# DLRM tower on one core: the first layer's dense part reads its features from the samples' slots instead of a contiguous copy

## The chip, the cores and the metric

One core of a Trainium2 chip. The metric is the device time of one launch in microseconds. Five engines work at once and meet only through semaphores: TensorE (PE, its weight loads listed apart as PEld), VectorE (DVE), ScalarE (ACT), GpSimd (POOL) and SyncE (SP, here only an issuer of transfers). 'us' is microseconds.

## What is computed

For each of 512 samples, 26 embedding rows of 128 numbers are looked up and put beside the sample's 128 dense features: 27 vectors. All pairwise dot products (351) and the dense features again go through three layers.

```python
combined = concatenate([e, dense[:, None, :]], axis=1)        # (512, 27, 128)
z = einsum('bfd,bgd->bfg', combined, combined)[:, triu_i, triu_j]   # 351 pairs
h = concatenate([z, dense], axis=1)                           # 479 features
h = maximum(h @ W_top1 + b_top1, 0)                           # 479 -> 512
h = maximum(h @ W_top2 + b_top2, 0)                           # 512 -> 256
y = h @ W_top3                                                # 256 -> 1
```

Everything is fp32.

## The kernel before

**Layout.** The samples go in four tiles of 128. `xt[d, tile, sample, slot]` holds the transposed vectors: on each of the 128 partitions (one for each feature number d), for each sample 32 slots of 4 bytes, of which 27 are used. Slot 0 is the dense vector, slots 1 to 16 the embeddings that are gathered from memory row by row, slots 17 to 26 those of ten small tables that are looked up by a matmul with a one-hot matrix. So the same slot of two neighbouring samples is 128 bytes apart. Within a tile a sample's place in `xt` is 4g + q, group inside quarter turned round: everywhere else (the transposed rows, the layers) it is 32q + g, with q in 0..3 and g in 0..31.

**The first half** (to about 58 us) is a loop over the ten one-hot tables (`for o in range(NO)` on every engine). The table comes by a transfer of SP (L267) into one of two buffers; the issue waits until DVE has finished with the table that was there (`low_ready`). ACT and DVE build the one-hot matrix out of PSUM (L375, L381, L476, L484). ACT rounds the table to its high part (L379), DVE makes the rest (L490), PE multiplies both (L627, L635), and ACT writes the picked 128 x 512 block into its slot of `xt` (L311). Meanwhile POOL issues 64 indirect gathers (L297). Behind the fourth table SP also issues the layers' weights, 1.5 MB (L272 to L277).

**The dense features** are loaded once (L270). PE transposes the four tiles into a PSUM bank behind the second table (L787). ACT, behind its work for the third table, copies the bank twice: into slot 0 of `xt`, turned into the order 4g + q (L394), and as it is into `dense_t`, 128 x 4 x 128 contiguous (L396). The second copy raises `dense_out`. PE waits for that before it uses the bank again, for the first transposes of gathered rows (`transposes`, L648).

**The second half** goes tile by tile, in an order written out by hand in PE's block (L796 to L836), with the other engines' lists beside it. For each tile: `transposes` (L650) turns gathered rows, ACT and DVE put them into `xt`; `gram` (L670) multiplies each pair of samples' slots with themselves, in four sets of 64 records; ACT (L325) and DVE (L523) take the results out; DVE transposes them by 32 x 32 blocks (L533), both pack the triangle's columns densely (`pack`, L355, L358, L540), PE transposes back (`back`, L693; for the last tile `back_last`, L706), ACT and DVE copy (L330, L545). Then come the first layer's 384 packed rows (`first_layer`, L726; `first_layer_last`, L712), the second (L737, L749) and the third layer (L762).

**The dense part** of the first layer, `dense_part(t, parts)`, L675 to L684, is what adds the 128 dense features: up to four matmuls of 128 x 128 x 128, one for each block of 128 outputs, with the weights `w1d_sb` stationary and the tile's dense features moving. It comes first in its PSUM region (`start`), the packed rows' matmuls add to it. Its calls stand as follows on PE, which keeps this order:

```python
gram(0)
pe.wait_ge(weights_in, WEIGHTS)
dense_part(0, (0, 1))
gram(1)
transposes(2, (0, 1))
back(0)
dense_part(0, (2, 3))
first_layer(0, range(N1 // P))
transposes(2, (2,))
dense_part(1)
second_layer(0)
```

For tile 2 it stands between `transposes(3, (0, 1))` and `second_layer(1)`, for tile 3 between `gram(3)` and the first half of `second_layer(2)`, behind which `back_last(2)` follows. For tiles 1 to 3 it waits until the layer's results of the tile before have left PSUM. The compiler makes two passes of each fp32 matmul, so two weight loads and two matmul records for each of the 16.

Of the kernel before, what the change touches and what calls it, by code (L numbers as in the profile page):

```python
# [23 lines left out]
P = 128  # L24
# [5 lines left out]
TILES = B // P  # L30
Q = 4
# [71 lines left out]
ACT = mybir.ActivationFunctionType  # L103
# [7 lines left out]
def tower(nc, dense, ids, ids_by_field, tables, w1_pairs, w1_dense, b1, w2, b2, w3, out):  # L111
    with ExitStack() as ctx:
        def sb(name, shape, dt=F32):
            return ctx.enter_context(nc.sbuf_tensor(name, shape, dt))

        def psum(name, shape):
            return ctx.enter_context(nc.psum_tensor(name, shape, F32))

        def sem(name):
            return ctx.enter_context(nc.semaphore(name))  # L120
# [2 lines left out]
        dense_sb = sb("dense_sb", [P, TILES, D])  # L123
        rows = sb("rows", [P, TILES, NG, D])
        xt = sb("xt", [P, TILES, P, PAD])
        dense_t = sb("dense_t", [P, TILES, P])
        gram_sb = sb("gram_sb", [P, NJ, G])
        pairs = sb("pairs", [P, NJ, PAD])
        packed = sb("packed", [P, NC * P])
# [5 lines left out]
        w1d_sb = sb("w1d_sb", [P, N1])  # L135
# [20 lines left out]
        tr_ps = [psum(f"tr_ps{i}", [P, 4, P]) for i in range(2)]  # L156
# [44 lines left out]
        dense_out = sem("dense_out")  # L201
# [103 lines left out]
        def _(act):  # L305
            act.dma_start(field_ids[:], ids_by_field).then_inc(field_ids_in, 16)

            def picked(o):

                act.wait_ge(pick_done, o + 1)  # L310
                act.activation(xt[:, :, :, NG + 1 + o], pick_ps[o % 2][:].rearrange("d (t p) -> d t p", t=TILES),  # L311
                               ACT.Copy).then_inc(pick_out, 1)

            def transposed(t, banks):
                for n in banks:
                    if n % 2 == 1:
                        act.wait_ge(tr_ready, TR_BEFORE[t] + n + 1)
                        act.activation(tile_slots(t, n), group_order(tr_ps[1], len(BANK_SLOTS[t][n])), ACT.Copy  # L318
                                       ).then_inc(tr_out_act, 1)
# [46 lines left out]
            def onehots(o):  # L366


                part = onehot[:, o % 2].rearrange("k c b -> k (c b)")[:, CHUNKS[o] * B - act_cols(o):CHUNKS[o] * B]
                act.wait_ge(ids_spread, o + 1)  # L370
                if o >= 2:
                    act.wait_ge(pick_done, o - 1)
                for c in range(shared(o), CHUNKS[o]):
                    at, cols = act_part(o, c)
                    last = act.activation(part[:, at:at + B - cols], ids_ps_act[o % 2][:, cols:], ACT.Abs,  # L375
                                          bias=row_neg[:, c:c + 1])
                last.then_inc(distance_ready, 1)
                act.wait_ge(table_in[o % TABLES], 16 * (o // TABLES + 1))
                act.activation(high[:, o % 2, 0:CHUNKS[o]], table[:, o % TABLES, 0:CHUNKS[o]], ACT.Copy).then_inc(high_ready, 1)  # L379
                act.wait_ge(distance_ready, o + 1)  # L380
                act.activation(part, part.bitcast(F32), ACT.Relu, scale=-1.0, bias=1.0).then_inc(onehot_act, 1)  # L381
# [5 lines left out]
            for o in range(NO):  # L387
                onehots(o)
                if o >= 1:
                    picked(o - 1)  # L390
                if o == 2:

                    act.wait_ge(dense_ready, 1)
                    act.activation(xt[:, :, :, 0].rearrange("d t (g q) -> d t g q", q=Q),  # L394
                                   tr_ps[0][:, :, :].rearrange("d t (q g) -> d t g q", q=Q), ACT.Copy)
                    act.activation(dense_t[:], tr_ps[0][:, :, :], ACT.Copy).then_inc(dense_out, 1)  # L396
                if o == NO - 3:
                    transposed(0, (1,))
                if o == NO - 2:
                    transposed(0, (3,))  # L400
# [195 lines left out]
        def _(pe):  # L596
# [78 lines left out]
            def dense_part(t, parts=range(N1 // P)):  # L675


                if t:
                    pe.wait_ge(h1_out_act, 2 * t)
                    pe.wait_ge(h1_out_dve, 2 * t)  # L680
                ps = h1_banks(t)
                for m in parts:
                    pe.matmul(ps[m], w1d_sb[:, m * P:(m + 1) * P], dense_t[:, t, :],  # L683
                              start=(m % 2 == 0 or t == TILES - 1), stop=False, skip_group_check=True)  # L684

            def back(t):
# [30 lines left out]
            def h1_banks(t):  # L717
                return h1_ps_last if t == TILES - 1 else h1_ps
# [79 lines left out]
# [11 lines that stand above are left out]
            back(1)  # L809
# [74 lines left out]
```

## Time and profile before

| | |
|---|---|
| median of 3 runs | 108.81 us (108.51 to 108.94) |
| the profiled execution | 108.96 us |
| its span, first to last instruction | 106.9 us |
| busy: PE / PEld / DVE / ACT / POOL | 99.4 / 78.6 / 79.8 / 76.7 / 63.6 us |
| granted PE clock | 1.00 in the whole span |
| transfers | 11.68 MB, mean 109 GB/s |
| dense part (L683) | 32 matmul records, 62.1 to 96.6 us |
| copy into slot 0 (L394) / into `dense_t` (L396) | 1154 / 643 ns |

The span is 2.06 us shorter than the execution's time; the rest lies before the first and after the last instruction. In a row of the groups or the timeline, out<-in are the program's names, then come partitions x elements. For matmuls the first shape is rows x columns of the weights; a matmul's duration includes its way through the array, so that neighbours overlap, and its end is modelled. What paces PE is therefore read from start to start.

### The profile page before, as it was taken

What the parts mean: (1) busy time and instruction counts of PE and PEld (TensorE: products, weight loads), DVE (VectorE), ACT (ScalarE), POOL (GpSimd) and SP (SyncE); (2) the same over time, 40 slices, a digit from 0 to 9 for tenths busy, and PEclk for the clock granted to TensorE, in tenths of its full rate; (3) what the DMA queues carried; (4) which work ended last, traced back from release to release, by engine and by line L of the source; (5) the groups of instructions that cost most, each with busy time, mean ns of one, the idle gap of its engine ahead of it and who ended that gap; (6) DMA issues with size and microseconds to landing.
All of it is one profiled execution on the core that took longest, in us unless ns stands there. A gap on an engine that the chain in (4) does not pass through costs nothing.

```text
span 106.9 us, 2530 instructions
## 1 busy us (share of the span) xinstructions
PE 99.4 (93%) x998; PEld 78.6 (74%) x998; DVE 79.8 (75%) x169; ACT 76.7 (72%) x149; POOL 63.6 (59%) x72
## 2 busy tenths in 40 slices
PE   5999999979799999999998999898999989999992
PEld 1246867555566668684787999797999979999991
DVE  6999999979799999999993599774117942587120
ACT  4499999998999999999975669541517661475430
POOL 3777777777777777777787777777777600000000
PEclk9999999999999999999999999999999999999999
DMA  3951458997736356364111111221121200000000
GB/s 51 357 197 49 89 205 237 380 341 233 253 60 244 90 207 192 110 199 144 55 49 49 49 55 55 64 58 49 49 55 49 55 25 0 6 0 0 6 0 1
DMA packets 5239, 11.68 MB, mean 109 GB/s; under 512 B 1998, under 2 KB 2520, under 8 KB 5228
## 3 DMA queue, kind: packets, MB, share of 16 engines
q1 hardware_dynamic: 3160, 7.31, 21.6%
q0 software_dynamic: 2048, 4.20, 13.1%
q8 instruction: 8, 0.13, 0.5%
q14 instruction: 3, 0.02, 0.1%
q10 hardware_dynamic: 20, 0.02, 0.1%
HBM read 11.48 MB, written 0.00 MB: 107 GB/s over the span
## 4 chain that ended last, share of the span: by engine, by line
PE 48%; DVE 22%; ACT 17%; DMA 6%; issue 4%; POOL 0%; POOLq 0%; DVEq 0%
PE gram_ps L670 14%; DVE onehot L476 12%; DMA table<-table 6%; ACT onehot L375 5%; PE top_ps L737 5%; PE tr_ps L650 5%; DVE low L490 5%; ACT xt L311 4%; PE act_ps L726 4%; ACT high L379 4%; PE dve_ps L726 4%; PE gram_ps L635 3%; ACT onehot L381 2%; PE gram_ps L627 2%; PE act_ps L683 2%
## 5 line engine op out<-in xcount | busy, mean ns | idle before, releaser
L297 POOL DMA_INDIRECT rows<-table,ids_sb x64 | 62.7, 980 | 20.7 <-issue 19.2
L627 PE MATMUL gram_ps<-onehot,high 128*128 128x512 f32 x82 | 21.5, 404 | 2.0 <-issue 1.8
L635 PE MATMUL gram_ps<-onehot,low 128*128 128x512 f32 x82 | 22.3, 408 | 0.4 <-DVE low L490 0.2
L627 PEld LDWEIGHTS gram_ps<-onehot,high 128*128 128x128 f32 x82 | 14.5, 188 | 6.9 <-issue 3.6
L635 PEld LDWEIGHTS gram_ps<-onehot,low 128*128 128x128 f32 x82 | 14.5, 188 | 6.3 <-DVE low L490 2.3
L490 DVE TENSOR_TENSOR low<-table,high 128x256 fp32r<-128x256 f32 (+1 forms) x40 | 16.6, 420 | 1.4 <-ACT high L379 1.3
L476 DVE TENSOR_TENSOR onehot<-gram_ps,row_f 128x1024 fp32r<-128x1024 f32 (+2 forms) x15 | 16.1, 1071 | 0.0
L476 DVE TENSOR_TENSOR onehot<-dve_ps,row_f 128x1024 fp32r<-128x1024 f32 (+1 forms) x15 | 15.4, 1031 | 0.0
L670 PE MATMUL gram_ps<-xt 128*58 128x52 f32 x512 | 14.7, 217 | 0.4 <-issue 0.3
L670 PEld LDWEIGHTS gram_ps<-xt 128*58 128x58 f32 x512 | 14.1, 133 | 1.1 <-issue 0.7
L523 DVE COPY gram_sb<-gram_ps 26x208 f32<-26x208 f32 x32 | 12.0, 376 | 3.0 <-PE gram_ps L670 2.0
L381 ACT ACTIVATE onehot<-onehot 128x1344 fp32r<-128x1344 f32 (+1 forms) x10 | 13.9, 1391 | 0.0
L311 ACT ACTIVATE xt<-gram_ps 128x512 f32<-128x512 f32 x10 | 11.5, 1151 | 2.2 <-PE gram_ps L635 2.2
L325 ACT ACTIVATE gram_sb<-gram_ps 26x208 f32<-26x208 f32 x32 | 10.7, 334 | 3.3 <-PE gram_ps L670 2.7
L379 ACT ACTIVATE high<-table 128x1024 fp32r<-128x1024 f32 (+1 forms) x10 | 11.2, 1120 | 0.7 <-DMA table<-table 0.7
L467 DVE COPY xt<-tr_ps 128x512 f32<-128x512 f32 (+1 forms) x9 | 6.1, 675 | 4.8 <-PE tr_ps L650 4.7
L375 ACT ACTIVATE onehot<-act_ps,row_neg 128x512 fp32r<-128x512 f32 (+1 forms) x15 | 8.4, 656 | 1.6 <-PE act_ps L602 1.6
L375 ACT ACTIVATE onehot<-top_ps,row_neg 128x512 fp32r<-128x512 f32 (+2 forms) x16 | 8.9, 665 | 0.0
L650 PE MATMUL tr_ps<-ident,rows 128*128 128x128 f32 x64 | 8.7, 275 | 0.0
L650 PEld LDWEIGHTS tr_ps<-ident,rows 128*128 128x128 f32 x64 | 7.3, 140 | 0.7
L318 ACT ACTIVATE xt<-tr_ps 128x512 f32<-128x512 f32 (+1 forms) x8 | 6.1, 762 | 2.1 <-PE tr_ps L650 2.0
L737 PE MATMUL top_ps<-h,w_sb 128*128 128x128 f32 x48 | 6.0, 275 | 0.0
(93 smaller groups left out, 107.7 us busy)
## 6 DMA issues: line engine op xcount, KB each, us to landing
table<-table SPq DMA_DIRECT2D x9, 512.0 KB, 3.7
rows<-table,ids_sb POOLq DMA_INDIRECT x64, 3.1
w1p_sb<-w_pairs SPq DMA_DIRECT2D x1, 768.0 KB
table<-table SPq DMA_DIRECT2D x1, 640.0 KB, 4.0
w_sb<-w SPq DMA_DIRECT2D x1, 512.0 KB
dense_sb<-dense SPq DMA_DIRECT2D x1, 256.0 KB, 5.1
w1d_sb<-w_dense SPq DMA_DIRECT2D x1, 256.0 KB
ids_sb<-ids SPq DMA_DIRECT2D x1, 52.0 KB, 1.9
```

The lines of the kernel that those rows point to most:

```text
L297: pool.indirect_dma_start(rows[:, t, s - 1, :], None, tables[f], bass.IndirectOffsetOnAxis(ids_sb[:, t, f:f + 1], 0)).then_inc(gathered[t] ...
L311: act.activation(xt[:, :, :, NG + 1 + o], pick_ps[o % 2][:].rearrange("d (t p) -> d t p", t=TILES), ACT.Copy).then_inc(pick_out, 1)
L375: last = act.activation(part[:, at:at + B - cols], ids_ps_act[o % 2][:, cols:], ACT.Abs, bias=row_neg[:, c:c + 1])
L379: act.activation(high[:, o % 2, 0:CHUNKS[o]], table[:, o % TABLES, 0:CHUNKS[o]], ACT.Copy).then_inc(high_ready, 1)
L381: act.activation(part, part.bitcast(F32), ACT.Relu, scale=-1.0, bias=1.0).then_inc(onehot_act, 1)
L476: dve.tensor_tensor(onehot[:, o % 2, cs[0]:cs[-1] + 1], ids_ps_dve[o % 2][:].rearrange("k (c b) -> k c b", c=1).to_broadcast(shape), row_f ...
L490: dve.tensor_tensor(low[:, b, piece], table[:, o % TABLES, piece], high[:, b, piece].bitcast(F32), ALU.subtract).then_inc(low_ready, 1)
L523: last = dve.tensor_copy(gram_block(s, q), gram_block_ps(t, s, q))
L627: pe.matmul(pick_ps[b][:], high[:, b, c, :], onehot[:, b, c, :], start=(c == 0), stop=False)
L635: last = pe.matmul(pick_ps[b][:], low[:, b, c, :], onehot[:, b, c, :], start=False, stop=(c == CHUNKS[o] - 1))
L650: last = pe.transpose(tr_ps[n % 2][:, s - slots[0], :], rows[:, t, s - 1, :], ident[:])
L670: last = pe.matmul(gram_ps[n % GRAM_BANKS][at:at + (HALF - 1) * PAD + NJ, k * HALF * NJ:(k + 1) * HALF * NJ], weights, pair[:, :, 1:N_SLOT ...
```

## The change

The buffer `dense_t` and ACT's copy into it go. The copy into slot 0 of `xt` now raises `dense_out`. The dense part's matmuls read slot 0 of the tile in `xt`, put into the order 32q + g by the access pattern: the outer step, over q, is 128 bytes, the inner one, over the 32 groups, is 512 bytes. Shapes, weights, order and count of the matmuls are the same.

```diff
-        dense_t = sb("dense_t", [P, TILES, P])
...
                     act.activation(xt[:, :, :, 0].rearrange("d t (g q) -> d t g q", q=Q),
-                                   tr_ps[0][:, :, :].rearrange("d t (q g) -> d t g q", q=Q), ACT.Copy)
-                    act.activation(dense_t[:], tr_ps[0][:, :, :], ACT.Copy).then_inc(dense_out, 1)
+                                   tr_ps[0][:, :, :].rearrange("d t (q g) -> d t g q", q=Q), ACT.Copy).then_inc(dense_out, 1)
...
                 for m in parts:
-                    pe.matmul(ps[m], w1d_sb[:, m * P:(m + 1) * P], dense_t[:, t, :],
+                    pe.matmul(ps[m], w1d_sb[:, m * P:(m + 1) * P], xt[:, t, :, 0].rearrange("d (g q) -> d q g", q=Q),
                               start=(m % 2 == 0 or t == TILES - 1), stop=False, skip_group_check=True)
```

## Rows read from the trace of the kernel before

**Rows 1.** The page: busy time of the engines, granted clock in 40 slices.
```profile
PE 99.4 (93%) x998; PEld 78.6 (74%) x998; DVE 79.8 (75%) x169; ACT 76.7 (72%) x149; POOL 63.6 (59%) x72
...
PEclk9999999999999999999999999999999999999999
```

**Rows 2.** Busy time of each engine in stretches (stretch, length, busy us, instructions).
```profile
core 0: us, PE busy (x) PEld busy (x) DVE busy (x) ACT busy (x) POOL busy (x), PEclk, DMA share, GB/s
...
62.10:95.70 33.60, 32.42 (x567) 30.64 (x562) 19.85 (x58) 17.51 (x58) 17.25 (x19) 1.00 0.14 39
95.70:106.90 11.20, 9.06 (x77) 8.60 (x75) 3.62 (x13) 4.00 (x16) 0.00 (x0) 1.00 0.01 2
```

**Rows 3.** Chain that ended last, in order of time (start us, us, what).
```profile
20.24 5.95 DMA table<-table
...
52.85 2.28 PE gram_ps L627 x10
...
92.19 3.55 PE gram_ps L670 x128
...
96.39 0.45 PE tr_ps L683 x4
```

**Rows 4.** Timeline of ACT, 17.9 to 26.3 us (start, us, line, operation, [idle before <-releaser]).
```profile
18.00 1.15 ACT L394 ACTIVATE xt<-tr_ps 128x512 f32<-128x512 f32 x1
18.93 0.64 ACT L396 ACTIVATE dense_t<-tr_ps 128x512 f32<-128x512 f32 x1
19.47 1.66 ACT L375 ACTIVATE onehot<-top_ps,row_neg 128x320 fp32r<-128x320 f32 x3
...
26.21 1.06 ACT L379 ACTIVATE high<-table 128x1024 fp32r<-128x1024 f32 x1 [0.48 <-DMA table<-table]
```

**Rows 5.** Timeline of PE's matmuls behind the dense part of tile 2.
```profile
84.65 0.61 PE L683 MATMUL dve_ps<-dense_t,w1d_sb 128*128 128x128 f32 x4
85.10 1.95 PE L737 MATMUL top_ps<-h,w_sb 128*128 128x128 f32 x16
```

**Rows 6.** Weight loads at 101.5 us; durations (min/median/max) of two lines.
```profile
101.49 0.53 PEld L762 LDWEIGHTS top_ps<-w_sb,h 128*128 128x128 f32 x4
...
L762 PEld LDWEIGHTS top_ps<-w_sb,h x2: 192/192/192, 101.5 to 101.6; 128*128 128x128 f32 x2
L762 PE MATMUL top_ps<-w_sb,h x1: 169/169/169, 101.6 to 101.6; 128*128 128x1 f32 x1
...
L683 PE MATMUL act_ps<-dense_t,w1d_sb x14: 275/275/377, 62.1 to 95.9; 128*128 128x128 f32 x14
```

**Rows 7.** Groups of ACT by shape (busy us, mean ns of one).
```profile
L325 ACT ACTIVATE gram_sb<-gram_ps 26x208 f32<-26x208 f32 x32 | 10.7, 334 | 3.3 <-PE gram_ps L670 2.7 <-issue 0.2
...
L335 ACT ACTIVATE pairs_t<-gram_ps 128x128 f32<-128x128 f32 x2 | 0.6, 277 | 0.9 <-PE gram_ps L706 0.9
```

**Rows 8.** Timeline, 61.5 to 69.5 us: second tile's Gram to the first layer.
```profile
62.78 3.90 PE L670 MATMUL gram_ps<-xt 128*58 128x52 f32 x128
64.71 3.16 DVE L523 COPY gram_sb<-gram_ps 26x208 f32<-26x208 f32 x8
66.61 1.09 PE L650 MATMUL tr_ps<-ident,rows 128*128 128x128 f32 x8
67.97 0.52 PE L693 MATMUL gram_ps<-ident,packed 128*128 128x128 f32 x3 [0.26 <-issue]
68.32 0.61 PE L683 MATMUL dve_ps<-dense_t,w1d_sb 128*128 128x128 f32 x4
...
68.52 0.38 ACT L330 ACTIVATE pairs_t<-gram_ps 128x256 f32<-128x256 f32 x1 [1.08 <-PE gram_ps L693]
68.96 1.60 PE L726 MATMUL act_ps<-pairs_t,w1p_sb 128*128 128x128 f32 x12
```

**Rows 9.** Timeline of PE at 96 us, behind the last tile's dense part.
```profile
96.67 1.06 PE L737 MATMUL top_ps<-h,w_sb 128*128 128x128 f32 x8
97.64 0.33 PE L706 MATMUL gram_ps<-ident,packed 128*128 128x128 f32 x1
```

## The prediction

> **What bounds the kernel now.** The page comes first: PE is busy 93% of the span, and the clock row grants it full speed, 2.4 GHz, in every slice [rows 1]. That is an average, so the stretches are read next. From 62.1 to 95.7 us PE works 32.4 of 33.6 us while DVE and ACT have two fifths or more of theirs free; only after 95.7 do waits between engines take a fifth of it [rows 2]. The chain of waits says the same: up to 58 us it runs through the one-hot lookups (DVE, ACT, one wait on a table's transfer), from there to the end nearly all of it is PE [rows 3]. The change touches both halves: it removes an ACT copy in the first, at 19 us, and changes what PE reads in the second, between 62 and 97 us.
>
> **The copy that goes.** ACT's copy into `dense_t` takes 0.64 us, but consecutive ACT operations overlap, and what it holds of the engine is from its start to the next start, 18.93 to 19.47: 0.54 us [rows 4]. Everything behind it on ACT moves up by that, up to the rounding of the table of the lookup after next. That operation starts at 26.21 after 0.48 us of idling, released by the table's transfer [rows 4]. The transfer was issued at 20.24 and took 5.95 us in the chain [rows 3]; what it waited for at its issue is DVE's work on the table in hand before, which depends on nothing behind the copy. So the idle time grows from 0.48 to 1.02 us and the 0.54 us are gone: **0 us** on the path. If that cover were missing (the table there by 25.7) the gain would be 0.54 at most. The next table's issue moves up by about as much, behind the same queue's earlier transfers; I cost it at nothing, since no ACT wait on that table shows later. `dense_out` is now raised by the first of the two copies; PE waits for it only ahead of the first embedding transposes, over 20 us later. No wait and no DMA is added, and no queue is passed.
>
> **What PE now reads.** Sixteen matmuls of the first layer (four tiles by four column blocks) take `dense_t` as moving operand. Each is two passes in the trace, a weight load and a matmul record each, so 32 passes. In `xt` the values of one tile's slot 0 lie 128 bytes apart, and in the order asked for (quarter outside, group inside) a step is 512 bytes. Nothing in this trace is read by PE with such a step; the price has to be bounded.
>
> What a pass costs now: sixteen passes of the same shape occupy 1.95 us from first start to last end, the last alone 0.275, so one starts every (1.95 - 0.275)/15 = 0.112 us [rows 5]. That pace is the weight load's: in the third layer, where only one column moves, four weight loads span 0.53 us with 0.192 for the last, again (0.53 - 0.192)/3 = 0.113 us [rows 6]. The columns go by underneath. Their own rate comes from the durations: 275 ns for 128 columns, 169 for one [rows 6] (ends of matmuls are modelled, so this is an indication), 106/127 = 0.835 ns for a value, 107 ns for a pass. Weights and columns are thus level at 107 to 112 ns, and there is **no spare room under the weight load** beyond some 5 ns: what slows the columns shows at once.
>
> *Lower bound.* Ten one-pass lookups of 512 columns take 2.28 us, 0.45 ns for a 4-byte value [rows 3], so contiguous values can be had almost twice as fast as these passes use them. And ACT reads PSUM with a step of 208 bytes for nothing: 208 elements in 334 ns against 277 for 128 contiguous, 0.71 ns for each further element [rows 7]. If SBUF gives PE one distant value in 0.83 ns, the change costs 0. A gain on PE is excluded: the weight loads stay.
>
> *Upper bound.* The only kind of operation with a 128-byte step in SBUF is ACT's write into `xt`: 1.15 us for 512 elements against 0.64 for the contiguous copy of the same bank [rows 4], 1.00 ns more for each. That added to 0.835 is 1.83 ns for a value. A pass of 128 such values is 234 + 5 = 239 ns, 127 more than now.
>
> I take the case in whole turns that this row is nearest to: a value that lies alone costs a second 0.835 ns. The pass becomes 2 x 107 + 5 = 218 ns, **0.107 us more**. A write isn't a read, but it is the one row about SBUF, and it has the same contiguous rate as the passes.
>
> The Trainium skill, SBUF — State Buffer, section "Specifications (TRN2)", says that SBUF works in 16-byte lines, that full bandwidth needs two or more hits in a line, and that each crossing to a new one has a penalty; it gives no figure for it. By that rule the change is slower and the free case, 108.8 us, is out; no row here shows it for a read, and ACT's write agrees with it.
>
> **What of it lies on the path.** Four groups of passes:
> - Tile 0, first two blocks (4 passes, +0.43 us). DVE's eight copies of the second tile's Gram sets run without a break from 64.71 to 67.87 and were held up by DVE's packing, not by PE; PE waits for them, 0.28 us within its second Gram (128 passes take from 62.78 to the next work at 66.61, 3.83 us, against 3.55 of the fourth tile's [rows 3]) and 0.26 us before the back-transposes at 67.97 [rows 8]. That is 0.54 us of slack: hidden, **0**.
> - Tile 0, last two blocks (4 passes, +0.43). They start at 68.32 and could hand over at 68.77; the first layer starts at 68.96, after ACT's copy that ends at 68.90 [rows 8]. Slack 0.19: **+0.24**.
> - Tiles 1 and 2 (8 passes each). PE goes from them straight into the second layer (tile 2 in [rows 5]), and ACT and DVE wait for its result: **+1.71**.
> - Tile 3 (8 passes, +0.86). Eight second-layer passes start at 96.67 and need 0.89 us, the back-transpose behind them starts at 97.64 [rows 9]: 0.08 us of waiting for ACT's packing absorbs that much, **+0.78**.
>
> Sum: 28 x 0.107 - 0.19 - 0.08 = **+2.73 us**. The profiled execution took 108.96 us (span 106.9 and 2.06 around it), 0.15 above the median 108.81; 111.69 on its terms, **111.5** on the median's. With 1.83 ns a value: 28 x 0.127 - 0.27 = 3.29, 112.1.
>
> **Rivals.**
> - *Free.* PE fetches a distant value in the 0.83 ns that it takes now, or prefetches. For: the lower bound above. Against: ACT's write. 108.8 us.
> - *Faster.* The table lands earlier than in this execution, ACT doesn't idle at 26.2, and the lookups that follow, which are ACT's in the chain, start up to 0.54 us sooner; PE is free as well. 108.81 - 0.54 = 108.2 or 108.3. It decides only if the landing comes before 25.7, 0.5 us earlier than shown, with the weights' 1.5 MB still ahead of it in the queue. Against: the DMA engines are the release named there, and nothing of theirs gets lighter.
> - *Fetched twice.* Each pass spends 0.835 ns on a value where the one-pass lookup spends 0.45, so it may walk its 128 columns twice rather than hold each for two turns. Then both walks pay 1.67 ns: 427 + 5 = 432 ns, +0.32 a pass. First group 1.28 - 0.54, the other 28 passes 8.97, less 0.27: +9.44, 118.2 us.
> - *No change in effect* is not open: the diff leaves no other source for the operand, and the weights are untouched.
>
> The Trainium skill, FP8 and Floating Point Precision, section "TensorE Precision Notes", counts four passes through the array for true fp32; with the two records of each matmul here that makes two to a record, and it leaves open whether they walk the columns twice. The trace's 0.835 against 0.45 ns agrees with two.
>
> **How the numbers follow.** Some 0.5% (0.54 us) is what a measurement of this kernel can tell. The change is slower by more when 28 d - 0.27 > 0.54, that is with d over 29 ns a pass. Chances: a pass slower by some 30 to 150 ns, 0.50 (its own range 109.4 to 112.5, most of it near 111.5); free 0.30; fetched twice 0.14; faster 0.06. The range leaves out the last two for the most part, 2 in 10, and takes in the free case and the upper bound of the price: 108.3 (108.8 less the runs' spread) to 112.5 (112.1 plus it). Slower 0.50 + 0.14 = 0.64, same 0.30, faster 0.06.
>
> **What would show it.** Right: the starts of the dense passes about 0.218 us apart instead of 0.112, weight loads waiting between them; the second tile's Gram without its 0.28 us wait; ACT's idle time before the 26.2 us operation near 1.0; every stage after 68 us later by the sums above, the dense part of the last tile starting 1.95 us later. Wrong: a pace of 0.112 (free), of 0.43 (twice), or a start of the lookup's ACT work at 26.2 that has moved, which would mean that the transfers, not the reads, changed the time.

## The result and the profile after

The changed kernel takes **111.78 us** (four runs, 111.33 to 112.20) against 108.83 beside it: ratio 1.0266, 95% interval 1.0243 to 1.0289, slower by 2.6 to 3.1 us. The forecast was 111.5. Measured once more beside other kernels (below), it took 111.43, ratio 1.0203 (1.0175 to 1.0231), 1.9 to 2.5 us. The runs of one and the same kernel spread by nearly 1 us, so the traces, stretch by stretch, tell more than the two medians.

From the page after; the lines answer to [rows 1]:

```profile
span 109.5 us, 2529 instructions
...
PE 102.1 (93%) x998; PEld 81.2 (74%) x998; DVE 79.7 (73%) x169; ACT 76.2 (70%) x148; POOL 63.7 (58%) x72
```

PE's busy time grew by 2.7 us with the same 998 records, ACT's fell by 0.5. The span went from 106.9 to 109.5. First the lookups: the timeline of ACT, to be laid beside [rows 4].

```profile
17.73 1.14 ACT L393 ACTIVATE xt<-tr_ps 128x512 f32<-128x512 f32 x1
18.68 1.65 ACT L374 ACTIVATE onehot<-top_ps,row_neg 128x320 fp32r<-128x320 f32 x3
...
26.25 1.06 ACT L378 ACTIVATE high<-table 128x1024 fp32r<-128x1024 f32 x1 [1.32 <-DMA table<-table]
```

The copy is gone, and the wait for the table took all of it: 1.32 us of idle time for 0.48, and the operation behind it starts at 26.25 for 26.21. (Of the 0.84 us, 0.54 are the copy; in this execution ACT was 0.27 us earlier even ahead of it.)

The chain that ended last, beside [rows 3]:

```profile
20.15 6.08 DMA table<-table
...
58.69 3.62 PE gram_ps L668 x128
62.31 1.05 PE act_ps L681 x4
63.36 3.55 PE gram_ps L668 x128
...
73.00 1.09 PE act_ps L681 x4
74.08 0.87 PE dve_ps L681 x4
74.96 1.79 PE top_ps L735 x16
...
98.70 0.87 PE tr_ps L681 x4
99.57 0.89 PE top_ps L735 x8
```

Four dense passes take 0.87 us of the chain where they took 0.45; second-layer passes, 16 in 1.79, are as they were. The pace of the dense passes themselves, on the timeline of PE around tile 2's and tile 3's, beside [rows 5] and [rows 9]:

```profile
86.12 1.05 PE L681 MATMUL dve_ps<-xt,w1d_sb 128*128 128x128 f32 x4
86.99 1.96 PE L735 MATMUL top_ps<-h,w_sb 128*128 128x128 f32 x16
...
99.39 1.07 PE L735 MATMUL top_ps<-h,w_sb 128*128 128x128 f32 x8
100.30 0.27 PE L704 MATMUL gram_ps<-ident,packed 128*128 128x128 f32 x1
```

From 86.12 to 86.99 four passes start: **0.218 us** each instead of 0.112. And around tile 0's two halves, beside [rows 8]:

```profile
62.24 1.12 PE L681 MATMUL act_ps<-xt,w1d_sb 128*128 128x128 f32 x4
...
63.29 3.62 PE L668 MATMUL gram_ps<-xt 128*58 128x52 f32 x128
64.81 3.15 DVE L521 COPY gram_sb<-gram_ps 26x208 f32<-26x208 f32 x8
...
68.06 0.52 PE L691 MATMUL gram_ps<-ident,packed 128*128 128x128 f32 x3
68.41 1.03 PE L681 MATMUL dve_ps<-xt,w1d_sb 128*128 128x128 f32 x4
...
69.27 1.52 PE L724 MATMUL act_ps<-pairs_t,w1p_sb 128*128 128x128 f32 x12
```

The second Gram starts 0.5 us later than before, runs without its wait, and DVE still sets the start of the back-transposes: 68.06 for 67.97, no later than the first half's own shift of 0.10. The first half of tile 0's dense part costs nothing. (A Gram is 128 records in the trace, 32 for each of its four sets, and not 64 for each, as the kernel's description has it.)

### The profile page after: what moved, and what is told of

Same layout as the page of the kernel before. It is cut to its first block, busy times and chain, and to the rows that moved or that the text cites. A ratio compares the mean times of both kernels' runs of the same rounds, so it can differ in the third digit from the quotient of the medians.

```text
span 109.5 us, 2529 instructions
## 1 busy us (share of the span) xinstructions
PE 102.1 (93%) x998; PEld 81.2 (74%) x998; DVE 79.7 (73%) x169; ACT 76.2 (70%) x148; POOL 63.7 (58%) x72
## 4 chain that ended last, share of the span: by engine, by line
PE 49%; DVE 22%; ACT 16%; DMA 6%; issue 5%; POOL 0%; POOLq 0%; DVEq 0%
PE gram_ps L668 13%; DVE onehot L474 11%; DMA table<-table 6%; ACT onehot L374 5%; PE top_ps L735 5%; PE tr_ps L648 5%; DVE low L488 4%; ACT xt L310 4%; PE act_ps L724 4%; PE dve_ps L724 4%; ACT high L378 3%; PE act_ps L681 3%; PE dve_ps L681 3%; PE gram_ps L633 3%; PE gram_ps L625 2%
## 5 line engine op out<-in xcount | busy, mean ns | idle before, releaser
L735 PEld LDWEIGHTS top_ps<-h,w_sb 128*128 128x128 f32 x48 | 6.0, 194 | 0.1
```

## The experiments

The theory: the read costs 0.106 us a pass, because each value lies alone in a 16-byte line, and the missing copy is worth nothing. The paces further down are each read from four or fewer passes of one traced execution. Rivals: the missing copy has a part in the time; the step's length (128 or 512 bytes) is what costs; any gap costs; each value is fetched twice.

**The read alone.** The copy stays, unread.

```diff
-                    pe.matmul(ps[m], w1d_sb[:, m * P:(m + 1) * P], dense_t[:, t, :],
+                    pe.matmul(ps[m], w1d_sb[:, m * P:(m + 1) * P], xt[:, t, :, 0].rearrange("d (g q) -> d q g", q=Q),
```

> ACT still makes the contiguous copy, nobody reads it, and the dense part reads slot 0 of xt. The read is the cause (mine): dense passes 0.218 us apart, time as the changed kernel, 111.8 us, ratio to before 1.027. Rival, the missing copy changed the transfers or the lookups and cost or gave part of it: 0.3 us or more away from the changed kernel, that is under 111.4 or over 112.2.

111.44 us, ratio 1.0218 (1.0188 to 1.0248). That was 0.3 us under the changed kernel, measured on another occasion, and left the first rival half alive. So both ran again beside each other, without an edit:

> The changed kernel once more, beside the same runs of the kernel before as the one that keeps the copy. Mine: the removed copy is worth nothing, so both have one ratio, about 1.023 to 1.026, within 0.3 us of each other; from the start of the first Gram to the end 48.8 us, as it was. Rival, the missing copy costs what lay between them so far: this one 0.3 to 0.4 us longer than the other, and that difference before the first Gram starts.

> Contiguous copy kept and unread, dense part from the slots, once more. Mine: the same ratio as the changed kernel. Rival: 0.3 to 0.4 us less.

The changed kernel: 111.43 us, 1.0203 (1.0175 to 1.0231). The copy kept: 111.37 us, 1.0208 (1.0178 to 1.0238). No difference: the 0.3 us were the spread between occasions. ACT's wait for the table shows the copy: 0.86 us without it, 0.55 with it, behind a slot copy that started 0.25 us later without it, which makes 0.56 together, and the operation behind the wait starts at 26.17 and 26.15. The chains say where the whole price is paid, from the start of the first Gram to the last operation. The kernel before:

```profile
58.59 3.62 PE gram_ps L670 x128
...
104.86 0.17 ACT y_sb L350
```

The changed kernel, again:

```profile
58.59 3.62 PE gram_ps L668 x128
...
107.36 0.17 ACT y_sb L349
```

and with the copy kept, again:

```profile
58.57 3.62 PE gram_ps L670 x128
...
107.34 0.17 ACT y_sb L350
```

48.77 us in both, 48.77 and 48.78 in the two earlier traces too, 46.27 in the kernel before. **The read costs 2.50 us**, and four traces agree on that to a hundredth. **The copy costs nothing** that these runs can tell: 0.06 us between the two medians, 0.02 between the starts of the first Gram. Other executions differ by more in that start, by 0.7 us (58.46 to 59.15) where no edit touches the lookups.

**Only tile 0 from the slots,** to test what slack hides.

```diff
-                    pe.matmul(ps[m], w1d_sb[:, m * P:(m + 1) * P], dense_t[:, t, :],
+                    pe.matmul(ps[m], w1d_sb[:, m * P:(m + 1) * P], xt[:, t, :, 0].rearrange("d (g q) -> d q g", q=Q) if t == 0 else dense_t[:, t, :],
```

> Both: contiguous copy kept, and only tile 0's dense part (8 of 32 passes) reads the slots. Mine: the first four passes are hidden by DVE's evictions, the next four cost 0.43 less 0.2 of slack: +0.2 us, 109.0. Rival, every pass is on the path: 8 x 0.107 = +0.86, 109.7.

109.11 us, ratio 1.0014 (0.9989 to 1.0040); the 0.86 is excluded. From the first Gram to the end it is 46.40 us (59.15 to 105.55), 0.13 more than before, by eight passes that each take about 0.105 longer. Both halves, on the timeline of PE:

```profile
62.70 1.12 PE L683 MATMUL act_ps<-xt,w1d_sb 128*128 128x128 f32 x4
63.75 3.62 PE L670 MATMUL gram_ps<-xt 128*58 128x52 f32 x128
...
68.88 1.04 PE L683 MATMUL dve_ps<-xt,w1d_sb 128*128 128x128 f32 x4
```

**More ACT copies,** to see how much the table's wait covers.

```diff
+        dense_u = sb("dense_u", [P, 2, TILES, P], BF16)
...
+                    for r in range(2):
+                        act.activation(dense_u[:, r], tr_ps[0][:, :, :], ACT.Copy)
```

> The kernel before with two more ACT copies of the dense bank (into a bf16 buffer nobody reads), about 0.54 us each of ACT's time, right behind the slot's. Mine, the wait for the table at 26.2 us covers 0.48 us of it and ACT sets the pace behind it: +0.6 us, 109.4. Rival, no cover, each ACT copy lies on the path: +1.08, 109.9, and the changed kernel's missing copy had gained 0.54. Rival, ACT is free there altogether: 108.8.

110.13 us in the median, ratio 1.0063 (1.0031 to 1.0095; it is nearer to the means than to the medians, which would give 1.011). Neither says much by itself, since there are two kinds of run: four with PE's mean granted clock at 1.0, 109.0 to 109.3 us, and eight at 0.984, 109.7 to 110.8. The profiled one is of the second kind. Its timelines of ACT and PE, and its stretches:

```profile
26.89 1.14 ACT L380 ACTIVATE high<-table 128x1024 fp32r<-128x1024 f32 x1
```

```profile
23.55 3.26 PE L630 MATMUL gram_ps<-onehot,high 128*128 128x512 f32 x8 [2.06 <-issue]
```

```profile
core 0: us, PE busy (x) PEld busy (x) DVE busy (x) ACT busy (x) POOL busy (x), PEclk, DMA share, GB/s
20.00:25.00 5.00, 2.94 (x12) 2.08 (x11) 3.23 (x6) 5.00 (x8) 3.77 (x4) 0.91 1.06 366
25.00:30.00 5.00, 5.00 (x18) 3.28 (x17) 3.87 (x9) 4.69 (x7) 3.92 (x4) 0.75 0.63 194
```

ACT's idle time at the table is gone, and the operation there starts at 26.89, 0.68 later than before: about the 0.6 expected. But PE had by then stood idle for 2.06 us, its clock fell to the lower level, and the next such operation comes at 31.98 for 30.80, 1.2 us later. The 0.6 us is confirmed at this one point of a trace; the runs at full clock show only 0.1 to 0.3 over the kernel before, and none of them was traced. At full clock the rival without cover (109.9) is excluded, but the one that ACT is free there altogether (108.8) is not. That the wait takes up the first part of an added copy is seen in the trace; what the rest costs is open.

**The cover taken away,** by letting the layers' weights queue behind the fifth table. The same edit in the kernel before and in the changed one.

```diff
-WEIGHTS_AFTER = 3
+WEIGHTS_AFTER = 4
```

> The kernel before with the layers' weights issued behind the fifth table instead of the fourth. The wait at 26.2 us should go: that table lands near 24, ACT has no idle time ahead of it, and the lookups end 0.48 us sooner: 108.4 (ratio 0.996). Rival, the weights then delay the sixth table past the 30.3 us at which ACT wants it, and the wait only moves: 108.8 or more.

> The changed kernel with the same later weights. If the table's wait is what makes the removed copy worthless, the copy's 0.54 us now comes back: 2.5 - 0.54 = 2.0 us longer than the kernel before with later weights, 110.4. Rival, the copy is worthless whatever the table does: 2.5 us longer, 110.9.

Before with later weights: 109.16 us, ratio 0.9989 (0.9963 to 1.0015). Changed with later weights: 111.64 us, 1.0234 (1.0192 to 1.0276). Both rivals came true by their numbers. The timeline of ACT in the second:

```profile
24.96 1.09 ACT L378 ACTIVATE high<-table 128x1024 fp32r<-128x1024 f32 x1
...
30.87 1.06 ACT L378 ACTIVATE high<-table 128x1024 fp32r<-128x1024 f32 x1 [1.18 <-DMA table<-table]
```

The fifth table comes in time and the operation on it starts 1.3 us earlier, but the sixth table now waits behind the weights, and ACT with it: 30.87, where it had been 30.86. The first Gram starts at 58.66. The 1.5 MB of weights have to pass somewhere, and whatever ACT gains ahead of them is given back there. So the total doesn't price the copy without cover; it shows that the cover moves along.

The profiled execution of the kernel before with later weights is one at a mean granted clock of 0.984, so its end is not compared. Up to 30 us its clock was full, and there it shows what the copy is worth as long as nothing covers it: from the start of the slot copy to that operation on the fifth table ACT takes 7.59 us with the copy (18.02 to 25.61) and 7.03 without it (17.93 to 24.96), 0.56 less. The sixth table's wait takes that back.

**Which gaps cost.** The contiguous copy is replaced by another layout in each tile; tiles 2 and 3 use the padding slots of `xt`, whose memsets stand early.

```diff
+        step8 = sb("step8", [P, P, 2])
+        step16 = sb("step16", [P, P, 4])
+        dense_t = [step8[:, :, 0], step16[:, :, 0], xt[:, 2, 0:P // 4, 28:32], xt[:, 3, 0:P // 2, 30:32]]
...
-                    pe.matmul(ps[m], w1d_sb[:, m * P:(m + 1) * P], dense_t[:, t, :],
+                    pe.matmul(ps[m], w1d_sb[:, m * P:(m + 1) * P], dense_t[t],
```

> Contiguous copy replaced by four layouts, one for each tile: tile 0 one value every 8 bytes, tile 1 one every 16, tile 2 four neighbours (16 bytes) every 128, tile 3 two neighbours (8 bytes) every 128. Time between starts of dense passes: by 16-byte lines with two values enough for full rate (mine) 0.112, 0.218, 0.112, 0.112 us. Rival, only far steps cost: 0.112 for tiles 0 and 1. Rival, any gap costs: 0.218 for tile 0 as well, and about 0.165 for tile 3. All four layouts' memsets of the padding stand early, so the total time is some 1 us longer for that and isn't the question.

The timeline of PE, tiles 0, 1, 2, 3 in this order, with what follows each:

```profile
69.53 0.62 PE L689 MATMUL dve_ps<-step,w1d_sb 128*128 128x128 f32 x4
...
74.92 1.08 PE L689 MATMUL dve_ps<-step,w1d_sb 128*128 128x128 f32 x4
75.83 0.85 PE L743 MATMUL top_ps<-h,w_sb 128*128 128x128 f32 x6
...
86.76 0.61 PE L689 MATMUL dve_ps<-xt,w1d_sb 128*128 128x128 f32 x4
87.21 1.95 PE L743 MATMUL top_ps<-h,w_sb 128*128 128x128 f32 x16
...
98.33 0.61 PE L689 MATMUL tr_ps<-xt,w1d_sb 128*128 128x128 f32 x4
98.78 1.05 PE L743 MATMUL top_ps<-h,w_sb 128*128 128x128 f32 x8
```

A value every 8 bytes: (0.62 - 0.275)/3 = 0.115 us a pass, nearly as contiguous. Every 16 bytes: (75.83 - 74.92)/4 = **0.227**. Four neighbours every 128 bytes: 0.112. Two neighbours every 128 bytes: (98.78 - 98.33)/4 = 0.112. At this pace neither the distance nor a gap matters by itself; whether a value has a neighbour in its 16 bytes does. A value alone costs 1.70 ns on the moving side of a matmul (0.218 us for 128). The Trainium skill, SBUF — State Buffer, section "Specifications (TRN2)", states the rule (two or more hits in a 16-byte line for full bandwidth), and this trace agrees for passes that use a value every 0.835 ns.

A second reading fits these rows as well: that every line costs some 1.7 ns, however many values it gives. With two values to a line that is 0.85 ns for each, just the pace of these fp32 passes; with four it is 0.43, and the lookups' contiguous columns take 0.45 [rows 3]. The two readings part for a pass that uses values faster than these do, from lines that give two each. No run here has one.

**Which steps cost.** The changed kernel with the order altered in three tiles, so that their dense sums are over other samples' features.

```diff
+                order = (xt[:, 0, 0:1, 0].to_broadcast([P, P]), xt[:, 1, :, 0],
+                         xt[:, 2, :, 0].rearrange("d (g q) -> d q g", q=2),
+                         xt[:, 3, :, 0].rearrange("d (g q) -> d q g", q=Q))
```

> The changed kernel with another order of the values in three tiles (so their sums are over other samples' features): tile 0 one and the same value 128 times (step 0), tile 1 step 128 bytes, tile 2 256, tile 3 512 as in the change. Time between starts of dense passes: a new 16-byte line for each value is what costs (mine): 0.112, 0.218, 0.218, 0.218 us. Rival, the 512-byte step meets the same bank: tile 1 and 2 clearly under 0.218. Rival, step 0 is as dear as any pattern that isn't contiguous: 0.218 in tile 0.

```profile
68.54 0.61 PE L684 MATMUL dve_ps<-xt,w1d_sb 128*128 128x128 f32 x4
...
73.91 1.06 PE L684 MATMUL dve_ps<-xt,w1d_sb 128*128 128x128 f32 x4
74.79 1.97 PE L738 MATMUL top_ps<-h,w_sb 128*128 128x128 f32 x16
...
86.13 1.05 PE L684 MATMUL dve_ps<-xt,w1d_sb 128*128 128x128 f32 x4
87.00 1.18 PE L738 MATMUL top_ps<-h,w_sb 128*128 128x128 f32 x9
```

One value 128 times: 0.112. Step 128: 0.220. Step 256: 0.218, and 0.218 for 512 (98.53 to 99.40 for four passes). With 0.227 for a step of 16 bytes, a longer step doesn't cost more, and the rival that a 512-byte step keeps meeting one bank is out.

**What sets the 1.7 ns.** Copy kept; tiles 0 and 1 load 64 of 128 weight columns (so half of the first layer's outputs lack the dense part), tiles 2 and 3 take the upper halves of values and weights as bf16, in one pass.

```diff
+                wide = P // 2 if t < 2 else P
+                near = (dense_t[:, t, :], dense_t.bitcast(BF16)[:, t, :].rearrange("d (n h) -> d n h", h=2)[:, :, 1])
+                far = (xt[:, t, :, 0].rearrange("d (g q) -> d q g", q=Q),
+                       xt.bitcast(BF16)[:, t, :, 1].rearrange("d (g q) -> d q g", q=Q))
+                feats = (near, far, far, near)[t][t // 2]
```

> Copy kept. Tiles 0 and 1 load only 64 of 128 weight columns (half of the first layer's outputs lack the dense part), tile 0 reads contiguous values, tile 1 the slots; tiles 2 and 3 read the upper two bytes of values and weights as bf16, in one pass: tile 2 from the slots, tile 3 with a step of 4 bytes. Time between starts: mine, in fp32 the columns alone take 107 ns a pass, so tile 0 stays near 0.107 though its weight load is half as long (0.056 if the columns were quicker than I took them), tile 1 0.214. In bf16 tile 2 tells what sets the 1.67 ns of a lone value: a fixed time for a line (mine) 0.214 us or more for its single pass; twice a column's own time: 0.107 or less; tile 3 0.112 or less.

```profile
68.59 0.65 PE L691 MATMUL dve_ps<-dense_t,w1d_sb 128*64 128x128 f32 x4
...
73.83 1.04 PE L691 MATMUL dve_ps<-xt,w1d_sb 128*64 128x128 f32 x4
...
85.38 0.60 PE L691 MATMUL act_ps<-xt,w1d_sb 128*128 128x128 bf16 x2
85.80 0.61 PE L691 MATMUL dve_ps<-xt,w1d_sb 128*128 128x128 bf16 x2
...
96.89 0.22 PE L691 MATMUL dve_ps<-dense_t,w1d_sb 128*128 128x128 bf16 x1
96.95 0.28 PE L691 MATMUL tr_ps<-dense_t,w1d_sb 128*128 128x128 bf16 x2
```

In tile 0 with half the weights the starts stand (0.65 - 0.323)/3 = 0.109 us apart (0.323 us is the last record alone): contiguous fp32 columns need their 107 ns by themselves, and weight load and columns are level, as taken. Tile 1, the same with the slots: (1.04 - 0.393)/3 = 0.216, with weight loads half as long. Tile 2, **one** pass over lone bf16 values: (85.80 - 85.38)/2 = 0.21 us, the same as an fp32 pass over lone values. Tile 3, bf16 with a step of 4 bytes and the same weights: 0.06. So a lone value costs a fixed 1.7 ns, whether the pass would otherwise use one in 0.835 ns or in about half of that. And an fp32 pass pays it once for each value: two fetches would take 0.43 us.

## Why the prediction was right

- *What goes: 0.* Right. The table's transfer takes the 0.54 us; with and without the copy the ratio is the same. Idle time of near 1.0 us was forecast; 1.32 came in one trace, 0.27 of it from an earlier start, and 0.86 in the other.
- *The price of a pass: 0.218 us, 0.107 more.* Right to a nanosecond, and that was luck in part: the bounds went from 0 to 0.127, and the middle case was a choice. It had a lone value cost a second turn of 0.835 ns. The bf16 pass contradicts that as a mechanism: a second turn would have taken it from 0.06 to some 0.11 us, and it takes 0.21. The price is a fixed 1.7 ns, which for fp32 happens to be two turns; whether more than chance lies in that is open. ACT's write was a good sign that a lone value in SBUF isn't free, but its own 1.00 ns extra would have given too much. The free case rested in part on ACT's reads of PSUM, which have a step for nothing; PE's reads of SBUF don't, and no run here tells whether engine or memory makes the difference.
- *No room under the weight load.* Right, and shown by the run with half the weights.
- *Fetched twice,* the rival at 118 us: wrong. The pace is 0.218 and not 0.43 us, and the single bf16 pass shows that even one walk over lone values takes 0.21.
- *Tile 0: 0 and +0.24.* Measured 0 and +0.21 (69.27 less 68.96, less the 0.10 that the lookups were late); with tile 0 alone 0.13 of it reached the end. The other 0.08 is slack that the forecast left out: PE's wait before the first layer, 0.19 us by the forecast, also made that layer start slowly. Before, its first weight load began only at 68.96, together with the first matmul, and the first twelve passes took 1.44 us (68.96 to 70.40); after, it began at 69.06, under the dense passes, and they took 1.35 (69.27 to 70.62).
- *Tiles 1 and 2: +1.71.* Measured from the dense start to the second layer's: +0.81 (74.78 - 73.00 against 73.74 - 72.77) and +0.84, 1.65. The term was 0.06 too high: tile 1's first four passes, which come behind a wait, grew by 0.39 us (72.77 to 73.29, now 73.00 to 73.91), the later groups of four by 0.42, where 0.43 was forecast.
- *Tile 3: +0.78.* +0.81 when the second layer starts (99.39), 0.75 at the back-transpose (100.30 - 97.58 against 97.64 - 95.67).
- *The sum: +2.73.* +2.50 in the trace, 0.23 less: 0.11 in tile 0, 0.06 in tiles 1 and 2, 0.03 in tile 3 and about 0.03 behind it. The last tile's dense part was forecast to start 1.95 us later and starts 1.81 later, counted from the first Gram. The medians differ by 2.95 and 2.3 us on two occasions, with the same 48.77 us behind the first Gram's start in the traces of both, so that the difference between the two lies outside the part that the read changes.

## What to carry to other kernels

Before a copy is dropped and its source read in place, see what else is under the reader: a copy that ACT makes while it would wait anyway costs nothing, and a step on PE's moving side is paid on the critical engine at each use. In fp32 the moving operand of these passes is free to lie apart as long as each 16-byte line gives two values; for a pass in bf16 or with one turn to a value that isn't shown. One value a line costs 1.7 ns, so compare that with the pass's own pace (here 112 ns for 128 columns). And time saved ahead of a wait for a transfer only makes the wait longer; if the transfers' order is changed, the wait may only move to the next buffer.

## What the runs showed that was not expected

- A bf16 pass over lone values is as slow as an fp32 one (0.21 against 0.218 us). Over bf16 values 4 bytes apart it takes 0.06, so lone values make it some three and a half times as long, where the fp32 pass only doubles.
- A step of 16 bytes is the dearest, 0.227 us a pass against 0.218 for 512 bytes. Why is open.
- The lookups stand close to a fall of the clock: one microsecond more of ACT's work at 19 us made PE idle for 2.06 us instead of 1.05, and in eight of twelve runs its mean granted clock fell to 0.984, with eight 512-column passes in 3.26 us for 2.13. The profiled run of the kernel before with later weights shows the same: PE idles for 1.84 us before 33.16, the next eight passes take 3.08 us, and the run's mean granted clock is 0.984. In the changed kernel an idle time of 1.55 us before 27.41 went by without a fall (2.13 us for the next eight).
